# Self attention on one core: q and k projected with features on the partitions, the sine multiply moved across partitions on VectorE

## The reference, cut to what matters

```python
q = (h @ wq + bq).reshape(b, s, H, HD).transpose(0, 2, 1, 3)      # H=16, HD=128, s=256, b=8
k = (h @ wk + bk).reshape(b, s, H, HD).transpose(0, 2, 1, 3)
v = (h @ wv + bv).reshape(b, s, H, HD).transpose(0, 2, 1, 3)
q = q * cos + _rotate_half(q) * sin        # rotate_half: (-x2, x1), halves of the 128 features
k = k * cos + _rotate_half(k) * sin
scores = einsum('bhqd,bhkd->bhqk', q, k) / sqrt(HD), causal mask, softmax
out = einsum('bhqk,bhkd->bhqd', probs, v) ... @ wo + bo
```

## Time and profile before

| | |
|---|---|
| runs | 2274.76 us median of 3 (2271.26 to 2274.86) |
| profiled execution | 2266.63 us, of which the span of instructions is 2264.7 us |
| TensorE (PE) busy | 1838.8 us, 81% of the span |
| VectorE (DVE) busy | 1126.6 us, 50% |
| ScalarE (ACT) busy | 1260.8 us, 56% |
| GpSimd (POOL) busy | 1057.5 us, 47% |
| mean granted TensorE clock | 0.922 |

### The profile page before, as it was taken

The page is one execution under the profiler, slowest core; times in us unless marked ns, Lnnn a source line. Parts: engine busy times, 40 slices in busy tenths (PEclk is TensorE's granted clock), DMA queues, the critical chain, the costliest instruction groups (busy, mean ns, idle before and its releaser), DMA issues.

```text
span 2264.7 us, 36408 instructions
## 1 busy us (share of the span) xinstructions
PE 1838.8 (81%) x11392; PEld 1605.2 (71%) x11392; DVE 1126.6 (50%) x3244; ACT 1260.8 (56%) x4119; POOL 1057.5 (47%) x1192
## 2 busy tenths in 40 slices
PE   3699998279999999999655554589888988888698
PEld 1487886158888888888555552478777877787598
DVE  1566665555555555555533332544444444444422
ACT  1367675236666666666522222387777777877321
POOL 2333332666657667655445553333333333333255
PEclk9799999589999999999877777699999999999799
DMA  3000000100000000000010000000000000000000
GB/s 102 17 15 15 15 24 19 60 31 15 24 16 15 29 15 15 15 15 10 5 33 16 16 8 28 20 10 8 9 10 10 7 10 10 17 12 17 3 15 24
DMA packets 29213, 42.81 MB, mean 19 GB/s; under 512 B 4704, under 2 KB 18528, under 8 KB 28768
## 3 DMA queue, kind: packets, MB, share of 16 engines
q1 hardware_dynamic: 29024, 40.48, 5.8%
HBM read 36.27 MB, written 4.19 MB: 18 GB/s over the span
## 4 chain that ended last, share of the span: by engine, by line
PE 52%; ACT 13%; DVE 11%; POOL 10%; issue 7%; DMA 1%; POOLq 1%; SPq 0%; ACTq 0%; DVEq 0%
PE pA L444 5%; PE pA L446 5%; PE pA L445 5%; PE pS L878 4%; PE pF L444 4%; PE pF L445 3%; PE pF L446 3%; ACT pA L1427 3%; ACT x_P L1461 3%; PE pF L610 3%; PE pO L897 2%; PE pS L589 2%; POOL moe_tb L1958 2%; PE pT L870 2%; PE pT L887 2%
## 5 line engine op out<-in xcount | busy, mean ns | idle before, releaser
L444 PE MATMUL pA<-Wh,XTh 128*128 128x512 f32 (+1 forms) x768 | 335.9, 437 | 22.3 <-POOLq L120 11.9
L446 PE MATMUL pA<-Wh,XTl 128*128 128x512 f32 (+1 forms) x768 | 292.1, 380 | 0.0
L445 PE MATMUL pA<-Wl,XTh 128*128 128x512 f32 (+1 forms) x768 | 291.5, 380 | 0.0
L439 POOL TENSOR_TENSOR Wl<-RAW,Wh 128x512 fp32r<-128x512 f32 (+3 forms) x96 | 101.9, 1061 | 288.2 <-ACT Wh L432 288.2
L444 PEld LDWEIGHTS pA<-Wh,XTh 128*128 128x128 f32 x768 | 148.8, 194 | 47.2 <-POOLq L120 13.1
L1176 POOL TENSOR_TENSOR f_t<-f_t,f_RB 128x512 f32<-128x512 f32 x128 | 165.0, 1289 | 16.7 <-DVE f_t L1060 16.6
L446 PEld LDWEIGHTS pA<-Wh,XTl 128*128 128x128 f32 x768 | 147.9, 193 | 28.7
L445 PEld LDWEIGHTS pA<-Wl,XTh 128*128 128x128 f32 x768 | 149.1, 194 | 21.1
L1060 DVE TENSOR_TENSOR f_t<-pA,f_sin 128x512 f32<-128x512 f32 x128 | 88.5, 692 | 140.7 <-PE pA L446 99.4
L986 ACT ACTIVATE f_P<-f_P,f_nm 128x128 f32<-128x128 f32 (+1 forms) x256 | 113.6, 447 | 49.6 <-DVE f_nm L1079 49.5
L1583 DVE TENSOR_TENSOR x_OTl<-pO,x_OTh 128x256 fp32r<-128x256 f32 x128 | 54.4, 425 | 169.6 <-ACT x_OTh L1475 169.3
(11 more groups left out here) (233 smaller groups left out, 5996.2 us busy)
## 6 DMA issues: line engine op xcount, KB each, us to landing
RAW<-in_w_f SPq DMA_DIRECT2D x32, 256.0 KB, 2.6
RAW<-in_w_x SPq DMA_DIRECT2D x32, 160.0 KB, 2.2
RAW<-in_w_x SPq DMA_DIRECT2D x32, 128.0 KB, 2.0
RAW<-in_w_ff SPq DMA_DIRECT2D x8, 288.0 KB, 2.8
R<-in_x SPq DMA_DIRECT2D x4, 512.0 KB, 5.8
x_spill<-R SPq DMA_DIRECT2D x1, 2048.0 KB, 7.6
f_bqk<-in_f_b SPq DMA_DIRECT2D x4, 512.0 KB, 3.9
RAW<-in_w_moe SPq DMA_DIRECT2D x8, 256.0 KB, 2.7
```

The source lines that it names most:

```text
L439: pool.tensor_tensor(Wl[slot][:, at], RAW[:, s, 0:cw], Wh[slot][:, at].bitcast(F32), ALU.subtract).then_inc(split_done, 1)
L444: e.matmul(o, ah, bh, start=first, stop=False)
L445: e.matmul(o, ah, bl, start=False, stop=False)
L446: return e.matmul(o, al, bh, start=False, stop=last)
```

## The change

It does five things, all in the self attention.

1. q and k are projected turned: the weights of one head (128 columns) are the stationary operand, and the 256 sequence rows are streamed. A projection n of q or k is now two heads (2 * (n // 2) and the next) of 256 columns each, in 12 matmuls of 128x256 rather than 6 of 128x512. The result has features on the partitions, which is the form of `qT` and `kT`.
2. The 16 transposes (`qk_tr`), their four copies on ScalarE (`qk_ev`) and the buffers `QR`, `KR` go. `qT` and `kT` have two buffers each.
3. The halves of a head are now on partitions 0 to 63 and 64 to 127. `take` does four `scalar_tensor_tensor` of 64x256 (bias added, multiplied by the sine), which read from one half of the partitions of PSUM and write to the other half of `sw`, and two of 128x256 with the cosine. Before, it was two `tensor_tensor` of 128x512.
4. The bias is a column per head in those instructions. The table of rotated biases and the two instructions a projection that used it go; GpSimd does one add of 128x512 for each q or k projection, rather than two. The 512 KB broadcasts of the q and k bias go; one small load at the start replaces them.
5. On VectorE `soft(i, 2)` now stands ahead of `take(j, 3)`.

```diff
                 def proj(i, n):
...
+                    b = slice((i % B) * S, (i % B + 1) * S)
+                    for a in range(2):
+                        o = pA[:, n % 2, a * S:(a + 1) * S]
+                        h = 2 * (n // 2) + a
+                        for k in range(KD):
+                            at = WK * (n % 2) + k * GW + h * HD
+                            w = slice(at, at + HD)
+                            xh, xl = XTh[:, k, b], XTl[:, k, b]
+                            e.matmul(o, Wh[g % 2][:, w], xh, start=(k == 0), stop=False)
+                            e.matmul(o, Wh[g % 2][:, w], xl, start=False, stop=False)
+                            ins = e.matmul(o, Wl[g % 2][:, w], xh, start=False, stop=(k == KD - 1))
                     ins.then_inc(q["proj"], 1)
...
                 def scores(i, h):
-                    e.wait_ge(q["te"], at_qk(i, NT - 1) + 1)
+                    e.wait_ge(q["rope"], NT * i + 2 * (h // 2) + 2)
...
             def dve(e):
...
                 def take(i, n):
-                    e.wait_ge(q["proj"], NQ * i + n + 1)
                     if n < 4:
                         m = NT * i + n
-                        x = (KR if n % 2 else QR)[:, n // 2, :]
+                        e.wait_ge(q["proj"], NQ * i + n + 1)
                         e.wait_ge(q["rope"], pos(m - 1))
-                        e.tensor_tensor(heads(t2[:, n % 2, :]), heads(pA[:, n % 2, :], True),
-                                        table(sinT, n // 2), ALU.mult).then_inc(q["rot"], 1)
-                        if i:
-                            e.wait_ge(q["tr"], at_qk(i - 1, n) + 1)
-                        e.tensor_tensor(heads(x), heads(pA[:, n % 2, :]), table(cosT, n // 2), ALU.mult
-                                        ).then_inc(q["taken"], 1)
+                        for a in range(2):
+                            h = (i // 8) * HG + 2 * (n // 2) + a
+                            for r in range(2):
+                                src, dst = slice(r * H2, (r + 1) * H2), slice((1 - r) * H2, (2 - r) * H2)
+                                e.scalar_tensor_tensor(sw[dst, n % 2, a, :], pA[src, n % 2, a * S:(a + 1) * S],
+                                                       bqk[src, n % 2, h:h + 1], sind[src, :], ALU.add, ALU.mult)
+                        e.wait_ge(q["sc"], pos(HG * (i - 1)))
+                        x = (kT if n % 2 else qT)[:, i % 2, 2 * (n // 2):2 * (n // 2) + 2, :]
+                        for a in range(2):
+                            h = (i // 8) * HG + 2 * (n // 2) + a
+                            ins = e.scalar_tensor_tensor(x[:, a, :], pA[:, n % 2, a * S:(a + 1) * S],
+                                                         bqk[:, n % 2, h:h + 1], cosd[:, :], ALU.add, ALU.mult)
+                        ins.then_inc(q["taken"], 1)
...
                 for i in range(NI):
                     j, k = i + 1, i + 2
                     one, two = j < NI, k < NI
+                    soft(i, 2)
                     if one:
                         take(j, 3)
-                    soft(i, 2)
-                    if one:
                         take(j, 4)
...
             def pool(e):
...
                 def rotate(i, n):
...
-                    e.tensor_tensor(y, y, RB[:, g % 2, n, :], ALU.add).then_inc(q["rotb"], 1)
-                    e.wait_ge(q["rotb"], m + 1)
                     e.wait_ge(q["taken"], NQ * i + n + 1)
                     e.tensor_tensor(x, x, y, ALU.add).then_inc(q["rope"], 1)
```

More of the change, by code:

```diff
@@ L855, in proj @@
                     e.wait_ge(q["taken"], pos(c - 1))
-                    t = n // 2 if n < 4 else n - 4
-                    w0 = WV if n >= 4 else WK * (n % 2)
-                    for k in range(KD):
-                        cc = slice(w0 + k * GW, w0 + (k + 1) * GW)
-                        ins = three(e, pA[:, n % 2, :], x_part(XTh, i, k, t), x_part(XTl, i, k, t),
-                                    Wh[g % 2][:, cc], Wl[g % 2][:, cc], k == 0, k == KD - 1)
-                    ins.then_inc(q["proj"], 1)
@@ L864, in qk_tr @@
-                def qk_tr(i, n):
-                    c = at_qk(i, n)
-                    e.wait_ge(q["te"], pos(c - 1))
-                    e.wait_ge(q["rope"], NT * i + n + 1)
-                    x = KR if n % 2 else QR
-                    for h in range(HG):
-                        ins = e.transpose(pT[:, c % 2, h * P:(h + 1) * P],
-                                          x[:, n // 2, h * HD:(h + 1) * HD], ident[:, :])
-                    ins.then_inc(q["tr"], 1)
+                    if n >= 4:
+                        for k in range(KD):
+                            cc = slice(WV + k * GW, WV + (k + 1) * GW)
+                            ins = three(e, pA[:, n % 2, :], x_part(XTh, i, k, n - 4), x_part(XTl, i, k, n - 4),
+                                        Wh[g % 2][:, cc], Wl[g % 2][:, cc], k == 0, k == KD - 1)
+                        ins.then_inc(q["proj"], 1)
+                        return
@@ L915, in pe @@
                     proj(0, n)
-                for n in range(NT):
-                    qk_tr(0, n)
                 proj(1, 0)
@@ L1006, in w_high @@
                     high_w(e, raw_in, q["hi"], cw_next if g == G - 1 else cw_here, i, i % 2, (g + 1) % 2)
-                for n in range(NT):
-                    qk_ev(0, n)
                 exp(0, 0)
@@ L1013, in act @@
                 for i in range(NI):
-                    j = i + 1
-                    one = j < NI
+                    j, k = i + 1, i + 2
+                    one, two = j < NI, k < NI
                     p_ev(i, 0)
@@ L1037, in act @@
                         normalise(j, 0)
+                    if one:
                         exp(j, 1)
@@ L1042, in dve @@
             def dve(e):
[L1043 to L1052 removed]
+                e.wait_ge(q["const"], 64)
@@ L1183, in w_low @@
                     low_w(e, q["hi"], q["split"], cw_next if g == G - 1 else cw_here, i, i % 2, (g + 1) % 2)
[L1185 to L1192 removed]
+                for i in range(2):
+                    for n in range(NT):
+                        rotate(i, n)
                 for i in range(NI):
[L1194 to L1196 removed]
                     w_low(i)
```

128 lines of the change are left out of this document (27 added, 101 removed).

## The result

The changed kernel takes 2318.36 us (median of 4 runs, 2317.02 to 2319.35); the kernel before, run beside it, takes 2273.01 (4 runs, 2267.23 to 2274.86). The ratio is 1.0204, 95% interval 1.0183 to 1.0224: slower by 45 us. The forecast was 2323.

A forecast was written before the change was run, and what follows sets the result against it. The prediction took the loop through VectorE to replace TensorE as the bound: rounds +58.8, start -11.4, end +0.6, +48 us on 2274.76 (8.1 above the profiled 2266.6), giving 2323 us. The 8-in-10 range was 2296 to 2356.

The forecast's parts named there:

- The bound and the loop: Self attention rounds: the order through VectorE, from proj(j, 5) to the next, sets a round of 21.7 us, against 19.74.
- P: Start of proj(j, 5) on TensorE, which needs take(j, 3); from there to take(k, 0) was forecast at 7.9 us.
- The three waits: TensorE waits for takes at proj(j, 5) about 1.6 us, proj(k, 3) 1.0, proj(j, 4) 1.2; together 3.85 a round.
- The take: Six VectorE instructions for a q or k projection: 2.72 us, or 2.80 behind another instruction; four make 11.1 a round.
- 10.6: The loop's us a round apart from four takes: 7.9 to take(k, 0), VectorE's o_low, soft and recip, and 0.14.
- Which starts are held: In a take, four half tiles and the first cosine multiply start without overlap, at 0.48 us; the others at 0.40.
- The start: Start of the self attention stage: first take at about 452, rounds beginning at about 475.4, 11.4 us earlier.
- The end: Last round of the self attention: 2.1 us of transposes lost but proj(j, 5) about 2.8 later, so +0.6 us.
- The clock: TensorE's clock in the rounds: new waits were taken not to lower it, so nothing was added.
- What costs nothing: GpSimd, with 4 adds a round, and ScalarE, below 12.4 us, do not hold TensorE; later stages stay the same.
- The half tiles overlap after all: Rival for the takes: 2.40 us each, a round 20.2, +2 us in all, 2277; chance 0.14.
- TensorE stays the bound: Rival for the rounds: with takes of 1.8 us or less, a round of 17.85, -71 us, 2204; chance 0.03.

The follow-up runs named there:

- Run 5: The changed kernel with take(j, 3) put back ahead of soft(i, 2) on VectorE: 2303.19 us, ratio 1.0141 to the kernel before.
- Run 2: The changed kernel with six whole 128x256 tiles a take, none changing partitions, two writing an unread buffer, halves not exchanged: 2253.26 us, ratio 0.9918 to the kernel before.
- run 3: The changed kernel with each half tile written to the half of the partitions it was read from, no swap: 2307.74 us, ratio 1.0163 to the kernel before.
- run 4: The changed kernel with half tiles reordered, both heads from the lower half, then both from the upper: 2291.56 us, ratio 1.0093 to the kernel before.
- Run 6: The changed kernel with work between takes spread evenly in three engines' lists and take(j, 3) ahead of soft(i, 2): 2369.53 us, ratio 1.0437 to the kernel before.
- run 1: The changed kernel with two whole 128x256 tiles replacing a take's four half tiles, halves not exchanged: 2200.68 us, ratio 0.9689 to the kernel before.
- run 12: The changed kernel with three wide tensor_tensor a take, biases kept through ScalarE and GpSimd, take(j, 3) ahead of soft(i, 2): 2200.94 us, ratio 0.9702 to the kernel before.
- run 9: The changed kernel with ScalarE copying q and k projections to SBUF, VectorE multiplying by sine, GpSimd by cosine and adding: 2294.05 us, ratio 1.0108 to the kernel before.
- run 8: The changed kernel with two 64x512 and one 128x512 tensor_tensor a take, q and k biases left out: 2222.26 us, ratio 0.9784 to the kernel before.
- run 7: The changed kernel with the evenly spread order and half tiles grouped by the half they read: 2316.24 us, ratio 1.0195 to the kernel before.
- run 11: The changed kernel in the evenly spread order, with ScalarE's o_ev(i, 3) moved ahead of exp(j, 1): 2279.42 us, ratio 1.0042 to the kernel before.

## Why the prediction was right

**The bound and the loop.** Right. The round closes through VectorE at proj(j, 5). From P to take(k, 0) it was 7.89 us, forecast 7.9, and VectorE goes without a pause from there to take(j + 1, 3). The three waits are where they were said to be: 1.57, 1.02 and 0.86 against about 1.6, 1.0 and 1.2. One term was wrong without any effect on the time: the waits sum to 3.45 rather than 3.85 although the round came out longer, so that TensorE is busy for 18.6 us of it (506.58 / 600 x 22.03), not 17.85. That sum only said where TensorE's own bound lies, which the loop exceeds either way. Run 5 moved the time by the one term it touched (0.58 a round for a `soft` of 0.55), and runs 2 to 4 by theirs, which they could not do if another engine set the round.

**The take.** Right in mechanism, a little small in size. Half tiles were taken at 0.48 each, alone; they are 0.50 apart (1.99 for four, against 1.92). The start behind `soft` was taken at 0.08 late; it is 0.12. So four takes are 4 x 2.78 + 3 x 0.12 = 11.5, where the sum had 11.1. With 10.6 this gives 22.1; measured are 22.0 in the round shown and 21.93 in the mean. Within the 10.6 two small errors cancel, which is luck: a reciprocal right behind another instruction takes 0.07 rather than 0.12 (801.60 to 801.67 here; the sum's 0.12 was read behind a wait), and P comes 0.23 behind the start of what follows the last take (808.95 to 809.18), not 0.14. The forecast 21.7 was 0.23 low, 30 x 0.23 = 7 us, the largest error of the sum (+65.7 against +58.8).

**Which starts are held.** The choice to price five starts of a take without overlap decided the forecast, and no row of the kernel before could show it. Run 2 shows the overlap of like instructions (0.395), run 3 that crossing is free and that a change of the output's start partition alone holds an instruction back, run 4 that each change costs 0.10. The rule of the Trainium skill that the prediction named (VectorE: DVE Perf Modes, section "Two Vector instructions with no wait between them") says the same of inputs and outputs; by it run 4 has two held starts fewer in a take, and a round 8 x 0.10 = 0.8 us less, and the trace agrees with 0.81.

**The start.** -11.0 against -11.4; the first take came at 452.85 (about 452), T(0) at 475.88 (475.4). **The end** +1.1 against +0.6. **The clock** stayed at 1.00 in the rounds, with waits of up to 1.57; the prediction took nothing for it. Run 6, with waits of 2.13 and matmuls at 1.2 GHz behind them, shows that this could not be taken for granted. **What costs nothing** held: ScalarE and GpSimd are in none of TensorE's waits.

**The sum.** Errors of both signs cancel, and part of the closeness of 2323 to 2318 is luck. The profiled execution was forecast at 2315 and is 2319.3: rounds, start and end are 7.8 us above their terms, and the stages behind, taken as the same, took 3.0 less in this execution. Then 8.1 us were added, the distance of before's median from its profiled execution; but that execution was a quick one of its kernel (2266.63, under all four of its times above), and the changed kernel's lies 0.9 above its median. Hence 2318.36 rather than 2323. A distance between one execution and a median should not have been carried over as a constant.

**The rivals.** *The half tiles overlap after all* was forecast at 2277; run 2, which makes the overlap true with six whole tiles, gives 2253, 24 us less. Its round is 19.87 against 20.2 (10 us of it), and its T(0) is at 472.18 rather than about 475 (3 us). In its profiled execution the stages behind took 7.5 us less than in that of the kernel before, and its median lies 5.0 above that execution rather than 8.1 (3 us). *TensorE stays the bound*, forecast at 2204, is what runs 1 and 12 show, at 2200.7 and 2200.9, with takes of 1.6 and 2.0 us; the condition given was 1.8 or less, and run 12 meets the time with 2.0 because, by the sum of the loop, `soft(i, 2)` is out of it: 10.6 - 0.55 + 4 x 2.02 is 18.1. Their rounds are 18.37 and 18.32, about 0.5 above the 17.85 of TensorE's work alone, of which 0.24 to 0.34 are the waits left; the rest was not followed further.

## What to carry to other kernels

When work is moved off the busiest engine, add up the loop through the engine that takes it over, from the buffer it frees to the next one, rather than its load: at 78% busy VectorE set the time here. On VectorE, half tiles that start at other partitions than the instruction in front cost more here than whole ones that do not; group those that start alike, make each as wide as it goes, prefer the operation that takes less for a column, and look at what stands directly behind an accumulator read. When an order is changed, look in the list of every other engine for the step that the new order now waits for: in run 6 it was one copy. Before an operand moves from PSUM to SBUF to relieve one wait, look at what GpSimd does at that moment.

## What the runs showed of the hardware that was not expected

- A `scalar_tensor_tensor` of 64x256 among changes of start partition takes 0.50 us from start to start, one of 128x256 among its like 0.395 (runs 2 and 4). A change costs 0.10 (run 4), and 0.12 behind an accumulator read, which is gone when the output starts where that read's does (run 3).
- A `tensor_tensor` of 64x512 with both inputs in SBUF lasts 0.69 us when no instruction of GpSimd's is under way at its start, also when one begins later, and 0.86 to 1.69 when one is (run 9); with one input in PSUM it lasts 0.69 beside GpSimd's adds (runs 8 and 12).
- A wait of 2.13 us, with one of 0.47 and 0.9 us of work ahead of it, was followed by 4.3 us of matmuls at a granted clock of 0.50 (run 6; 0.87 over the stage). With waits of 1.93 and 0.27 at the same places the mean was 0.92 (run 7), with a single one of 1.90 it was 0.99 (run 11), and with none above 1.57 it was 1.00 (the change). So the longest wait alone does not tell what the clock does.
